# A two-layer adapter kernel on one core: order of loads and stores in the slots of its first batch

## The reference, cut to what matters

```python
x = x + einsum('bnr,bor->bno', einsum('bni,bri->bnr', x, B0[ids]), A0[ids])    # first layer, rank 16
logits = einsum('btd,ed->bte', x, Wr) + bias          # 8 experts
gates = softmax of the two largest logits, else 0
h = einsum('btd,erd->bter', x, A)                      # rank 16 for each expert
x = x + einsum('btd,od->bto', x, W) + 2.0 * einsum('bter,bte,eor->bto', h, gates, B)
```

## Time and profile before

| | us |
|---|---|
| three runs | 1646.81, 1650.13, 1650.48 |
| median | 1650.13 |
| the profiled execution, its own time | 1652.38 |
| its span from first to last instruction | 1650.5 |
| PE busy | 1591.0 (96%) |
| DVE busy | 1187.2 (72%) |
| ACT busy | 750.9 (45%) |
| mean granted TensorE clock | 0.986 of full |

### The profile page before, as it was taken

One profiled execution on the slowest core, in us unless ns is written; L12 is line 12 of the kernel. 1 busy time (PEld: TensorE's weight loads), 2 busy tenths in 40 slices (PEclk: granted clock), 3 DMA queues, 4 the chain that ended last, 5 costly groups with the idle time before them and its releaser, 6 DMA issues.

```text
span 1650.5 us, 21070 instructions
## 1 busy us (share of the span) xinstructions
PE 1591.0 (96%) x7680; PEld 1336.1 (81%) x7680; DVE 1187.2 (72%) x1615; ACT 750.9 (45%) x984; POOL 9.7 (1%) x19
## 2 busy tenths in 40 slices
PE   7897988899999999999999999999999999999998
PEld 5785867778888888888888888888888888888887
DVE  3674444379769877788769877788769877787665
ACT  4552332335444545445444545445444555445443
POOL 1100000000000000000000000000000000000000
PEclk9898999999999999999999999999999999999999
DMA  8577666668978798868878798868878798566664
GB/s 246 161 239 202 193 175 190 207 190 238 226 196 235 213 240 206 217 227 219 219 193 239 215 236 208 214 229 221 218 194 236 218 239 205 192 223 210 205 220 161
DMA packets 414776, 351.30 MB, mean 213 GB/s; under 512 B 284698, under 2 KB 329034, under 8 KB 413642
## 3 DMA queue, kind: packets, MB, share of 16 engines
q1 hardware_dynamic: 412498, 345.77, 74.7%
q10 hardware_dynamic: 2176, 4.19, 0.9%
HBM read 280.62 MB, written 68.82 MB: 212 GB/s over the span
## 4 chain that ended last, share of the span: by engine, by line
PE 89%; SPq 3%; DMA 2%; DVE 2%; ACT 2%; issue 1%; ACTq 0%; DVEq 0%
PE pb L786 26%; PE pb L787 26%; PE pb L788 26%; PE pb L369 4%; PE pb L371 3%; PE pb L523 2%; SPq L648 2%; DMA raw<-in_L_cond_W_dram 2%; PE pb L672 1%; SPq L305 1%; DMA wrn<-in_L_cond_Wr_dram 1%; DVE whl L775 0%; ACT xa L343 0%; DMA t_scr<-tst 0%; DVE pool_a L530 0%
## 5 line engine op out<-in xcount | busy, mean ns | idle before, releaser
L771 ACT CAST whl<-raw 128x1024 fp32r<-128x1024 f32 (+1 forms) x440 | 460.3, 1046 | 645.3 <-PE pb L788 645.2
L775 DVE TENSOR_TENSOR whl<-raw,whl 128x1024 fp32r<-128x1024 f32 (+1 forms) x440 | 535.0, 1216 | 286.3 <-ACT whl L771 286.1
L786 PE MATMUL pb<-whl,sh 128*128 128x512 f32 x1568 | 612.9, 391 | 0.5 <-DVE ost L824 0.5
L787 PE MATMUL pb<-whl,sh 128*128 128x512 f32 x1568 | 611.6, 390 | 0.0
L788 PE MATMUL pb<-whl,sl 128*128 128x512 f32 x1568 | 611.2, 390 | 0.0
L788 PEld LDWEIGHTS pb<-whl,sl 128*128 128x128 f32 x1568 | 294.3, 188 | 62.9
L786 PEld LDWEIGHTS pb<-whl,sh 128*128 128x128 f32 x1568 | 294.5, 188 | 56.2 <-DVE whl L775 0.9
L787 PEld LDWEIGHTS pb<-whl,sh 128*128 128x128 f32 x1568 | 294.6, 188 | 55.0
L369 PE MATMUL pb<-awb,xa 128*128 128x304 f32 x512 | 138.5, 304 | 2.9 <-DVE aux L384 1.6
L371 PE MATMUL pb<-awb,xa 128*128 128x256 f32 x512 | 134.4, 280 | 0.0
L786 PE MATMUL pb<-whl,xh 128*128 128x512 f32 x256 | 110.1, 430 | 3.3 <-DVE ost L824 1.9
(11 more groups left out here) (142 smaller groups left out, 1321.9 us busy)
## 6 DMA issues: line engine op xcount, KB each, us to landing
raw<-t_scr SPq DMA_DIRECT2D x392, 512.0 KB, 4.2
xst<-in_x_dram SPq DMA_DIRECT2D x896, 32.0 KB, 3.6
raw<-in_L_cond_W_dram SPq DMA_DIRECT2D x128, 128.0 KB, 2.7
t_scr<-tst SPq DMA_DIRECT2D x32, 512.0 KB, 4.3
raw<-bt_scr SPq DMA_DIRECT2D x28, 512.0 KB, 3.7
out_dram<-ost SPq DMA_DIRECT2D x28, 512.0 KB, 4.2
out_dram<-u SPq DMA_DIRECT2D x28, 512.0 KB, 3.4
t_scr<-raw SPq DMA_DIRECT2D x8, 512.0 KB, 3.1
```

The costliest lines, as they stand in the source:

```text
L771: e.copy(pair_split(w_high, g), pair_source(g)).then_inc(c_wh, 1)
L775: e.tensor_tensor(out=pair_split(w_low, g), in0=pair_source(g), in1=pair_split(w_high, g).bitcast(f32), op=ALU.subtract).then_inc(c_wl, 1)
L786: e.matmul(o, h, part(w_high, g, k), start=start, stop=False)
L787: e.matmul(o, h, part(w_low, g, k), start=False, stop=False)
```

## The change

Three moves, all in the slots of batch 0; no operation is added or removed.

```diff
@@ act_main
                 for u in DELTAS0.get(i, ()):
                     first_hi(e, u)
-                if 9 <= i < 25:
-                    x_hi(e, 1, i - 9)
                 if i == 26:
                     bx_hi(e, 1)
...
                 if more:
                     w_keep(e, i + 3, 1)
+                if 9 <= i < 25:
+                    x_hi(e, 1, i - 9)
@@ dve_main
                 if i:
                     pair_lo(e, i + 1)
+                if 10 <= i < 26:
+                    x_lo(e, 1, i - 10)
                 if i == 4:
                     aux_final(e, 0)
...
                 if i == 7:
                     hg_lo(e, 0)
-                if 9 <= i < 25:
-                    x_lo(e, 1, i - 9)
@@ sp_main
             for i in range(SLOTS0):
-                if i + 2 < SLOTS0 and (i + 2) % 9 != 8 and w_number(i + 2) % 2:
-                    w_sums_store(e, i + 2)
-                if i == 3:
-                    bt_store(e)
-                    bt_difference_store(e)
                 if i == 4:
                     first_load(e, 9)
                     first_load(e, 8)
                 elif i + 5 < SLOTS0 and i != 3:
                     first_load(e, i + 5)
+                if i == 3:
+                    bt_store(e)
+                    bt_difference_store(e)
+                if i + 2 < SLOTS0 and (i + 2) % 9 != 8 and w_number(i + 2) % 2:
+                    w_sums_store(e, i + 2)
```

## The result

| | before | after |
|---|---|---|
| median, us | 1650.02 (4 runs, 1646.81 to 1650.48) | 1661.12 (4 runs, 1659.54 to 1664.91) |
| ratio after to before, 95% interval | | 1.0075, 1.0053 to 1.0096 |
| profiled execution, own time | 1652.38 | 1664.91 |
| its span | 1650.5 | 1663.0 |
| mean granted clock | 0.986 | 0.984 |

What follows compares the result with a forecast made beforehand. Batch 0 was taken as the place to look, with PE waiting for loads and DVE for stores. Terms 0.5 + 2.4 + 1.5 + 2.4 + 1.2 = 8.0 us slower, forecast 1658.1, own range 1654 to 1663, 8 in 10 1641 to 1666.

Steps and rivals of the forecast that it cites:

- The gain: Slots 10 and 21: loads come early enough to save two waits and two clock falls, 11.5 us if nothing else is late.
- The held store, slot 5: Slot 5's store queues behind the load of tile 10, so SP's later transfers lag 2.1 us, between 0.90 and 3.3.
- Slot 3: The store follows the two bt stores and one w_sums waits a little: 0.5 us, between 0 and 2.1.
- Slot 10: x_lo behind w_sums' wait for the store: small products of unit 0 at 165.0, net 0.5 us later; clock fall left out.
- The edge: Slots 11 to 15 and 22 to 24: x_lo just after pair_lo comes slightly late, 2.4 us in all, between 0 and 4.
- Slots 16 to 21: SP lags again; unit 11's products in slot 21 wait for x_lo behind x_turn, 1.5 us, plus a clock fall, 2.4.
- Slots 26 to 31: Slot 28's store lands last, so slot 30's turn is 1.7 later, 0.5 caught up: 1.2 us, between 0 and 1.7.
- The gain stands: Rival: the store lands before about 157.5 in slot 9, w_sums doesn't hold x_lo, 9.4 us gained, 1640.7; chance 0.2.
- It evens out: Rival: SP's lag is only 0.9 and no new clock fall comes; 1652, no change within 5 us; chance 0.28.
- more is slower: Rival: a clock fall also after slot 10 and SP's lag at its upper bound, 12.8 us slower, 1663; chance 0.12.

Runs made afterwards that it cites:

- the kernel with three stores behind: The kernel before, with only the stores of slots 5, 14 and 23 issued behind the load: 1654.17 us, ratio 1.0025.
- the kernel with the late slots as before: The changed kernel, with the stores from slot 26 on ahead of the loads as before: 1658.73 us, ratio 1.0055.
- SP's mixed list: The kernel before, load ahead of store except in slots 3, 5, 14, 23 and from 26: 1645.66 us; with x_hi, x_lo as in the change 1655.18.
- the best one with the identity first: Kernel before, x_lo ahead of w_sums, load first except slots 3, 5, 14, 23, add_identity of tile 33 ahead of w_sums in slot 29: 1644.68 us.

## Why the prediction was right, and where its sizes were off

The forecast, 1658.1 with slower as the likeliest case, had the right sign and, for slots 9 to 15, the right mechanism; the time is 3.0 us above it, inside the range. For slots 16 to 21 and for the end the sum is near the measured one partly by luck. Step by step, by the table of starts:

**The gain.** The loads of slots 10 and 21 came in time, as forecast. That it isn't seen in the time is shown to be the collision and the held stores: with both taken away the same order of SP gives 1645.7, a gain of 4.4 us. The 11.5 "if nothing is late next" and the rival's 9.4 were in no version. The two falls of slots 10 and 21 are gone in that kernel's trace, as forecast, but other things are late: PE waits for `x_lo` from its old place too, 1.64 us in slot 10 and 1.05 in slot 21, it waits 2.00 before the turn of slot 19 where before waited 0.66, and a fall stands in slot 30 where before had none. With `x_lo` ahead of `w_sums` the gain is 5.1.

**The held store, slot 5.** Forecast 2.1 us of lag (the sum that is given for it makes 2.17). From the load of tile 10 to the next load SP took 8.2 us instead of 5.9, and slot 9 came 2.6 later than slot 7 did. Right, and alone it was seen in the kernel with three stores behind. For all three stores the price was 4.1.

**Slot 3.** Forecast 0.5. The distance from slot 4 to slot 6 is 13.18 us before and 13.80 after; it is 13.77 to 13.88 in the kernels that share the order of slot 3 and 13.19 to 13.26 in those that don't. 0.6.

**Slot 10.** Forecast: PE waits about 3.3 us for `x_lo` at 165.0. It waited 2.21, since it came there later: slot 9's longer wait, 4.05, had a fall of the clock behind it (the stretch of 155.43), where before had its one in slot 10. The net from slot 7 on was 0.2 later against a forecast of nothing beyond slot 3's 0.5. **The fall behind this wait was left out of the likeliest sum, and it came**: 1.7 us. This is the first mis-sized term. The ground given was that 3.42 and 3.23 us idle had brought a fall and 2.35 had not; the fall of 90.58, 0.6 us behind an idle time of 2.19 us in a place where before had 1.13, shows that this ground doesn't hold, and so does a wait of 2.81 us in slot 9 with no fall (last section). PE's timeline there:

```profile
89.98 0.66 PE L1091 MATMUL pb<-ident,xst 128*128 128x128 f32 x4 [2.19 <-ACT bt L1100]
```

**The edge.** Forecast 2.4 us for the eight slots: measured 1.0 in slots 11 to 14 and 1.1 in 22 to 24, 2.1 in sum. The kernel with this move alone lost 2.7 in its median. Right.

**Slots 16 to 21.** Forecast 1.5 for the products of unit 11 and 2.4 for the fall; from the turn of tile 18 on, 1.2 and 1.7 were added. That is near, but not by the forecast's steps. The lag of SP was there: from the load of tile 19 to the next one 8.2 us instead of 5.9. Where it bit was slot 17, which the forecast didn't look at: PE waited 2.88 us for `x_lo` behind `x_turn`, and the clock fell in slot 18 behind an idle time of 2.27 us that was 1.89 before and had none. Less 0.7 regained in slot 16, these two made 4.4 us by the small products of slot 18. Against them stand 4.7 won until the turn of tile 24, its 3.23 and the smaller waits of slots 19 and 20 (0.66 and 0.53), all gone. In slot 21 itself `x_lo` waited behind `w_sums` for the store until 263.71, the mechanism of slot 10, and `x_turn` behind it had no wait for its data, which the forecast had as the cause. The sum came out by luck.

**Slots 26 to 31.** Forecast 1.2, the second mis-sized term. From slot 29 to the end 4.2 us were lost: 2.2 more of waiting in slot 30, then 2.8 in a stretch at half clock, with 0.7 regained later. The step that failed is "the turn is 1.7 later; 0.5 of that is caught up by DVE", with "no fall" taken for granted behind it. The wait itself was 0.5 larger than said. The fall isn't the change's alone: behind waits of 2.31 us and of 2.08 in the same slot the clock fell too, in the kernel with the late slots as before and in the one with x_lo and x_hi moved alone, and in all it fell in seven of the eight kernels that waited 2.06 to 2.32 us there. The profiled execution of before, with 2.11, was the one that escaped it. From slot 29 to the end the kernel with the late slots as before lost 0.9 us against before, so of the 4.2 some 3.3 hang on the order of these slots. Against it 1.9 us were gained in slots 25 to 28, which no step had: a wait of 0.7 us in slot 28 is gone, and of the half-clock stretch around slot 25 more lay in the idle time of 5.77 us.

**The start.** 1.4 us of the 12.5 were there before any moved instruction and 1.2 more at the fall of 90.58, in slot 1, where the change moves one store behind a load. The kernel with three stores behind, whose slots 0 to 4 are those of before, came to the turn of tile 3 at 74.41 and had a fall at 90.53 too, and the others came to it between 72.6 and 74.7 whatever their lists. So these 2.6 us belong to the execution. That they are also in the median isn't said by that: a profile is one execution, and its terms are good to an us or two.

**The rivals.** *The gain stands* named the condition: the store must land before about 157.5 in slot 9. It landed at 164.06 here, in a slot that began 6.0 later, so 158.1 by the old time. It failed, though by little. *It evens out* and *more is slower* were judged by falls of the clock. Between 110 and 360 us before has five stretches at half clock, 30.7 us, and after has eight, 37.6 us; five of after's, in slots 9, 10, 18, 21 and 30, have none of before's at their place, and before's two behind the waits for the loads of tiles 13 and 24 are gone. The time fell between the forecast and the latter's 1663. The rule of the Trainium skill, "DMA: Bandwidth & Descriptors", Queues, rings and completion order, that an engine takes descriptors in ring order, agrees with the traces in slot 8: before, DVE was released by the store at 156.84 and PE by the load at 158.55; after, PE had the load by 162.52 and DVE the store at 164.06. The load's gain and the store's loss are both there. The slow issue behind a store, which the prediction gave for it, says nothing of the order.

## What to carry to other kernels

Before a load is put ahead of a store in one queue, look for who waits for the store to land, and then for what stands behind that waiting instruction on its engine. Look also at what else the queue sends behind the store, here x of the next batch, whose late landing cost a wait of 2.88 us in slot 17. Here the engine that waited was idle half of the time, and the wait was harmless until one short operation with a close deadline stood behind it. A move that cost 2.7 us alone cost 9.5 beside another that was itself a gain, so try moves apart and together. A list of exceptions (here slot 3, the three slots whose load itself waits, and those from 26 on) may hold the whole gain: the same order on SP alone gave 0.27% slower in all slots and 0.26% faster in the slots where the load was free to go. And a wait that is taken from in front of one instruction on an engine in order turns up in front of the next that someone needs.

## What the runs showed of the hardware

An idle time's length doesn't decide alone whether TensorE's clock falls behind it. Two kernels with nearly the same idle time in the same slot, one stretch each, the first that with `x_lo` as in the change and SP's mixed list:

```profile
148.07 1.09 PE L672 MATMUL pb<-ident,raw 128*128 128x128 f32 x4 [2.66 <-DMA raw<-in_L_cond_W_dram]
...
147.43:150.84 3.41, 2.77 (x9) 2.42 (x10) 3.37 (x6) 1.11 (x2) 0.00 (x0) 0.50 0.59 145
```

and the second the best one with the identity first:

```profile
148.61 0.63 PE L672 MATMUL pb<-ident,raw 128*128 128x128 f32 x4 [2.81 <-DMA raw<-in_L_cond_W_dram]
...
147.43:150.84 3.41, 2.21 (x11) 1.77 (x12) 2.82 (x6) 1.97 (x3) 0.00 (x0) 1.00 0.49 88
```

2.66 us idle, ended at 148.07, and the clock was at 0.50 (1.2 GHz) around it; 2.81 us, ended at 148.61, and it stayed at 1.00 (2.4 GHz). The longer one had no fall. They lay half a microsecond apart; that this is the reason isn't shown. Slot 30 shows it again, with the kernel in which only x_hi and x_lo are moved and so the same work there as before. First its turn and the stretch behind it, then such a stretch of before:

```profile
326.29 0.30 PE L672 MATMUL pb<-ident,raw 128*128 128x128 f32 x1 [2.08 <-DMA raw<-in_L_cond_W_dram]
...
326.65:330.06 3.41, 3.41 (x11) 2.73 (x10) 1.86 (x3) 0.69 (x2) 0.00 (x0) 0.50 0.97 327
```

```profile
330.16:333.58 3.42, 3.42 (x18) 2.91 (x19) 2.23 (x3) 0.69 (x2) 0.00 (x0) 1.00 0.94 326
```

2.08 us idle there and half clock, 11 matmuls in the stretch; 2.11 in before, full clock, 18. The Trainium skill, "TensorE: Matmul & The Clock Gate", What's actually happening, says that the monitor that sets this clock runs free and isn't reset by a kernel's start; these rows fit that and don't prove it. So a wait of 2 to 3 us had a fall behind it, some 2 us more, in some of the profiled executions and not in others, and a forecast should carry it as a chance on each such wait, not as a threshold.

Second, the same fall costs more or less by how much of its half-clock stretch lies in the idle time itself: the turn of tile 28 came 0.9 us into the stretch that began at 290.81 before, and 3.0 us into that of 298.79 after, which is 2.2 us less at half clock, by an estimate 1.1 us of time. The table of starts has 1.0 us regained from that turn to the small products of the same slot (297.68 and 306.84).
